# A two-layer attention kernel in one core: the engines' loop of 13 trips is written out

## The reference

```
# layer 0
h = group_norm(x, 32 groups) * gn_w + gn_b
q, k, v = split(qkv_w @ h + qkv_b)          # 128 channels each
a = softmax(q^T k / sqrt(128))              # 1024 x 1024 for each image
x = x + proj_w @ (v a^T) + proj_b
# layer 1
q, k, v = Wq @ x + bq, Wk @ x + bk, Wv @ x + bv   # q, k: 16 channels, v: 128
out = gamma * (v softmax(q^T k)^T) + x
```

## Time and profile before

| | |
|---|---|
| time, median of 3 runs | 1760.5 us (1756.99 to 1760.75) |
| time of the profiled execution | 1758.94 us |
| its span, first to last instruction | 1757.2 us |
| mean granted TensorE clock | 0.964 of full |
| PE busy | 1565.0 us (89%) |
| DVE busy | 1345.7 us (77%) |
| POOL busy | 1252.4 us (71%) |
| ACT busy | 1218.9 us (69%) |

### The profile page before, as it was taken

How to read it: one execution, slowest core, us unless ns; L and a number is a source line. 1 busy time by engine, 2 the same in 40 slices (tenths; PEclk the granted TensorE clock), 3 DMA queues, 4 the chain that set the end, 5 groups by cost and what they waited for, 6 DMA issues and landing times.

```text
span 1757.2 us, 47297 instructions
## 1 busy us (share of the span) xinstructions
PE 1565.0 (89%) x16777; PEld 1170.5 (67%) x16777; DVE 1345.7 (77%) x2547; ACT 1218.9 (69%) x1697; POOL 1252.4 (71%) x1039
## 2 busy tenths in 40 slices
PE   4889999898989989898998989989899898999965
PEld 2567777676767767676766767767676676776654
DVE  2578888787878878788787878878788787888853
ACT  2477777676767767677676767767677676777753
POOL 6997778677777878677676767868678676777600
PEclk9999999999999999999999999999999999999986
DMA  2699999999998999999899999999999999999964
GB/s 56 121 176 192 191 195 190 166 197 171 190 194 163 191 178 194 165 195 190 153 201 164 191 186 166 192 165 199 160 192 189 161 194 165 191 182 189 182 119 90
DMA packets 1081092, 305.20 MB, mean 174 GB/s; under 512 B 1067952, under 2 KB 1068624, under 8 KB 1080912
## 3 DMA queue, kind: packets, MB, share of 16 engines
q1 hardware_dynamic: 1079760, 302.41, 95.6%
q10 hardware_dynamic: 1152, 0.00, 0.0%
HBM read 17.13 MB, written 16.78 MB: 19 GB/s over the span
## 4 chain that ended last, share of the span: by engine, by line
PE 47%; ACT 22%; issue 14%; DVE 13%; POOL 2%; DVEq 1%; DMA 0%; ACTq 0%; SPq 0%; POOLq 0%
DVE nmax L499 9%; PE mixed L704 8%; PE mixed L706 7%; PE mixed L705 7%; ACT prob L404 7%; ACT scores L409 7%; PE scores L665 4%; PE scores L690 4%; PE bank_w L772 3%; PE bank_t L725 3%; PE scores L667 3%; PE scores L666 3%; ACT k_odd L438 2%; ACT v_head L456 2%; PE bank_w L762 2%
## 5 line engine op out<-in xcount | busy, mean ns | idle before, releaser
L704 PE MATMUL mixed<-v_head,pt 128*128 128x129 f16 x4096 | 746.1, 227 | 66.5 <-issue 63.8
L705 PE MATMUL mixed<-v_tail,pt 128*128 128x128 f16 x4096 | 745.1, 223 | 0.0
L706 PE MATMUL mixed<-v_head,pt 128*128 128x129 f16 x4096 | 745.1, 224 | 0.0
L499 DVE TENSOR_REDUCE nmax<-scores 128x1 f32<-128x1024 f32 x512 | 603.0, 1217 | 68.1 <-PE scores L690 46.9
L312 POOL TENSOR_TENSOR rows<-prob,rows 128x1024 f16<-128x1024 f32 x256 | 545.1, 2129 | 21.3
L409 ACT ACTIVATE scores<-scores,nmax 128x1024 f32<-128x1024 f32 x256 | 278.6, 1088 | 330.4 <-DVE nmax L499 330.4
L307 POOL TENSOR_SCALAR rows<-prob 128x1024 f16<-128x1024 f32 x256 | 267.9, 1046 | 310.7 <-ACT prob L404 308.9
L704 PEld LDWEIGHTS mixed<-v_head,pt 128*128 128x128 f16 x4096 | 408.5, 100 | 72.2 <-issue 67.7
L513 DVE SCALAR_TENSOR_TENSOR rows<-scores,rows 128x1024 f16<-128x1024 f32 x256 | 313.6, 1225 | 149.6 <-ACT rows L416 149.6
L705 PEld LDWEIGHTS mixed<-v_tail,pt 128*128 128x128 f16 x4096 | 415.5, 101 | 2.6 <-issue 0.3
L706 PEld LDWEIGHTS mixed<-v_head,pt 128*128 128x128 f16 x4096 | 407.1, 99 | 0.0
(11 more groups left out here) (93 smaller groups left out, 1927.2 us busy)
## 6 DMA issues: line engine op xcount, KB each, us to landing
x_raw<-in_x_dram SPq DMA_DIRECT2D x32, 512.0 KB, 4.9
out_dram<-y SPq DMA_DIRECT2D x64, 256.0 KB, 2.7
pt<-rows SPq DMA_TRANSPOSE x512, 4.6
w_qkv<-in_L_conv_qkv_w_dram SPq DMA_DIRECT2D x3, 64.0 KB, 3.8
w_proj<-in_L_conv_proj_w_dram SPq DMA_DIRECT2D x1, 64.0 KB, 3.7
w_v<-in_L_conv_Wv_dram SPq DMA_DIRECT2D x1, 64.0 KB, 3.6
b_qk<-in_L_conv_bk_dram SPq DMA_DIRECT2D x4, 0.1 KB, 2.4
b_qk<-in_L_conv_bq_dram SPq DMA_DIRECT2D x2, 0.1 KB, 3.1
```

What stands on the lines that cost most here:

```text
L499: nc.vector.reduce_max(nmax[layer][:, t:t + 1], scores[layer][:, :], AX.X, negate=True).then_inc(maxed[layer], 1)
L704: mm(mixed[l][:, 0:C + 1], head, vh[:, im.p, m, 0:C + 1], start=(m == 0), stop=False)
L705: mm(mixed[l][:, 0:C], head, vt[:, im.p, m, :], start=False, stop=False)
L706: done = mm(mixed[l][:, 0:C + 1], tail, vh[:, im.p, m, 0:C + 1], start=False, stop=(m == TILES - 1))
```

## The change

The loop on the engines goes away. `every_iteration` now writes all iterations from -1 to 34 out, so that each engine's program holds all of them; image numbers are constants everywhere. The order of the instructions on each engine and all waits stay as they are in the source. SP, POOL, ACT, DVE and PE all call the new form.

```diff
-LOOP = (2, 15)
...
-def every_iteration(engine, body):
-    for it in range(FIRST_IT + 1, 2 * LOOP[0]):
-        body(whole(it))
-    with engine.Fori(LOOP[0], LOOP[1]) as pair:
-        body(Image(pair, 0))
-        body(Image(pair, 1))
-    for it in range(2 * LOOP[1], LAST_IT + 1):
+def every_iteration(body):
+    for it in range(FIRST_IT + 1, LAST_IT + 1):
         body(whole(it))
...
-            every_iteration(pe, body)
+            every_iteration(body)
```

More of the change, by code:

```diff
@@ L271, in _ @@
                 sp.dma_start(b1_qk[r:r + CQK, :], col(src)).then_inc(setup_loaded, 16)
-            every_iteration(sp, body)
+            every_iteration(body)
             for h in range(2):
@@ L393, in _ @@
             body(whole(FIRST_IT))
-            every_iteration(pool, body)
+            every_iteration(body)
         @block.scalar
@@ L492, in _ @@
             act.wait_ge(consts_made, 10)
-            every_iteration(act, body)
+            every_iteration(body)
         @block.vector
@@ L657, in _ @@
             setup()
-            every_iteration(dve, body)
+            every_iteration(body)
         @block.tensor
```

## The result

The kernel with everything written out takes 1682.16 us in the median of four runs (1680.64 to 1683.96), against 1760.62 us before, the median of four runs too. The ratio is 0.9556, with a 95% interval of 0.9535 to 0.9577. The forecast was 1684, from 1675 to 1698.

What follows compares the result with a forecast made beforehand. PE, with 89% busy the leading engine, was held up by 12 taken jumps of its loop; 26 x 49.45 = 1285.7 for 1361.1, 75.4 us less, gave 1683.5 for the profiled execution and 1684 as forecast, range 1675 to 1698.

Steps and rivals of the forecast that it cites:

- A taken jump on PE costs 6.6 us: At PE's loop branch, line 84: each taken jump costs 6.6 us, clock included, 79.3 us for 12.
- the place is innocent: End of every second iteration on PE: the taken branch costs, not the place; the fall-through there idles only 0.28 us.
- The step of the sum: PE's 12 jumps go: 12 x 6.6 = 79.3 us come off the path that sets the end.
- The split of the 6.6 us: Each PE jump: about 5.6 us idle, the rest of the 6.6 from the slow restart.
- the slow restart: PE after each stop: granted clock at 0.50 for about 4 us, adding something over 1 us to each jump.
- Written-out iterations take 49.45 and not 49.30: Former loop's 26 iterations: 0.15 us slower each, 3.9 us in all, seemingly from line 672's separate wait before layer 0's scores.
- More fetches for the other four cost nothing: ACT, DVE, POOL, SP: up to 72 more q14 packets, hidden; rival: mild 1691 to 1705, full 2015, most of slower's 0.05.
- The DMA queue: Rival: DMA becomes the limit, mild 1689 to 1710, full near 1759; shares 0.11 for mild losses, 0.03 for no change.
- The clock: Rival: PE's full clock not granted so long without pauses, near 1696; shares 0.11 with mild queue and fetch losses.
- the estimate from the 108 ns: Rule against the forecast: 12 compare-and-branches at about 0.108 us, 1.3 us for the whole change; rejected for PE's trace.
- The median: Whole kernel: profiled execution 1683.5 us, median 1.6 above it at 1685, set at 1684.

Runs made afterwards that it cites:

- e1: Only PE written out, SP, POOL, ACT and DVE keep their loops, against the kernel before: 1681.11 us, ratio 0.9551.
- e3: All five engines loop over a body of four iterations with six trips, five jumps on PE instead of 12: 1712.81 us, ratio 0.9727 to the kernel before.
- e5: Everything written out, plus 12 two-trip loops of one semaphore increment on PE where the jumps were: 1685.66 us, ratio 0.9576 to the kernel before.
- e2: Only PE keeps its loop, the other four engines are written out, against the kernel before: 1750.38 us, ratio 0.9951.
- e6: The kernel before, with its loop, without the matmuls of `attend` on `v_tail`, so PE's body has 1727 instructions: 1727.58 us.
- e9: Everything written out, then four-trip loops of semaphore increments, 100 to 1100 on PE and 100 to 700 on ACT; branch durations were read, no total time given.
- e7: Everything written out, without the matmuls of `attend` on `v_tail`: 1668.12 us.
- e4: The changed kernel with PE's wait for `exped` ahead of those for `x1_done` and `y_done` in some steps: 1678.30 us, ratio 0.9532 to the kernel before.
- e11: The changed kernel with PE's `exped` wait moved ahead, measured again beside the changed kernel on one chip: 1676.68 us, ratio 0.9528 to the kernel before.
- e12: Only PE written out, with its `exped` wait moved ahead, the other four engines loop: 1678.22 us, ratio 0.9529 to the kernel before.

## Why the prediction was right

**A taken jump on PE costs 6.6 us, and the place is innocent: right, shown.** PE alone gives the gain (e1), five jumps cost about in proportion (e3: 1712.8 - 1682.2 = 30.7 us more than the changed kernel; with 24 x 0.15 = 3.6 us that its looped iterations save, 34.3 for five, 6.9 each by the medians, 7.6 each in its trace), and branches to code at hand take 0.23 us at most (e5). The step of the sum was 79.3 us for 12. So 6.6 us is the mean of this kernel's 12 jumps and no fixed price: in its own trace they cost 4.9 to 7.5 us. The forecast took that mean from the very jumps that were to go, and it needed no more.

**Its parts.** The stop is a fetch: bodies too large to stay at hand are brought anew, and packets arrive within it (e2, e6, e9). The split of the 6.6 us, 5.6 for the stop and "the rest" for the slow restart, was mis-sized, which the total hides. PE's busy time fell by 25.2 us, 2.1 for each jump, where I had said 1 to 2. The 8 us behind the restart at the first, second and sixth jump of the kernel before, in the windows view (columns as in the earlier trace rows), show it directly:

```profile
313.15:321.15 8.00, 7.99 (x66) 6.72 (x67) 1.27 (x3) 1.21 (x3) 5.41 (x5) 0.68 1.15 183
417.96:425.96 8.00, 7.99 (x86) 6.73 (x87) 2.41 (x4) 2.02 (x4) 6.04 (x5) 0.83 1.03 178
836.32:844.32 8.00, 7.99 (x74) 6.73 (x75) 1.71 (x4) 1.32 (x4) 4.08 (x4) 0.74 1.03 183
```

At a mean granted clock of 0.68, 8 busy us are short of 0.32 x 8 = 2.6 us of work; at 0.83 it is 1.4, at 0.74 it is 2.1. The first two jumps isolate the clock: their stops are alike (4.3 and 4.4 us), and the iterations behind them take 55.40 and 54.37 us (the first is in the earlier trace rows). Of the 1.2 us between the two losses of work, 1.0 shows in the time.

The idle time before the first load is 5.55 us in the mean of the 12 and the work lost at half clock 2.0; together 7.5, of which 6.6 show. The other 0.9 us seems to be taken up by PE's own ordinary waits. An iteration without a jump has 2.1 us in which PE is not busy (47.22 busy of 49.30), and in the one behind the first jump the scores' weight loads waited for the exponential for 1.6 us, where it was 2.6 in the one before. For each of the 12 jumps, and for those of e2 and e3, the trace gives the same sum, idle time plus lost work (half of the time at the lower level) less 0.9 to 1.0 us; e3's 7.6 us are 5.8 and 2.7 less 0.9.

In e6 PE has 7.8 us of such waits (40.98 busy of 48.80). Its loop costs 59.5 us, to which 26 x 0.17 = 4.4 come for e7's slower written-out iterations (48.96 us against 48.79): in all 63.9, 5.3 for each jump. Its trace has 5.25 us of idle time and 1.8 of lost work for each, so 1.8 us is taken up there. So the slow restart costs about 2 us of work after each stop, and how much of that and of the stop reaches the time is a matter of PE's slack.

**Written-out iterations take 49.45 and not 49.30: right, and its cause shown.** 1285.64 us for 26, with 1285.7 in the sum. The cause, a wait met last that sits one instruction ahead of the weights load, was called "seems"; e4 and e11 moved that wait and got iterations of 49.30 us, which is 31 x 0.14 = 4.3 us by their number; the medians fell by 3.9 and 6.3. This is the one part of the change that works against it.

**More fetches for the other four cost nothing: right but for one stop.** q14 went to 70 packets, where I had said 91 or fewer; q8 to 135 (137). The price is not quite nothing. In the changed kernel one iteration takes 49.72, and ACT's timeline has a stop that the iteration before has not:

```profile
1199.41 1.09 ACT L403 ACTIVATE scores<-scores,nmax 128x1024 f32<-128x1024 f32 x1 [1.50 <-DVE nmax L493]
1200.87 1.02 ACT L410 ACTIVATE rows<-scores 128x1024 f16<-128x1024 f32 x1 [0.37 <-ACT scores L403]
```

```profile
1149.97 1.09 ACT L403 ACTIVATE scores<-scores,nmax 128x1024 f32<-128x1024 f32 x1 [1.50 <-DVE nmax L493]
1151.15 1.02 ACT L410 ACTIVATE rows<-scores 128x1024 f16<-128x1024 f32 x1
```

Line 410 follows line 403 by 1.46 us in place of 1.18. This 0.28 us came, in this same iteration, in every kernel here in which all engines are written out, and in neither of the two in which PE alone is and ACT keeps its loop (e1, e12). It is what a fixed boundary in ACT's code would do; that it is one was not tested.

**The rivals.** The DMA queue did not become the limit: at a share of 1.09 it kept 49.45 for 26 iterations, and `attend` waited no more than before. The clock was granted for 1286 us on end. And the estimate from the 108 ns that the Trainium skill ("Advanced Engine Details and Errata", Control Flow Timing) gives for a compare-and-branch, 1.3 us in all, was off by the factor 60 for these jumps; the branches of ACT (45 ns) and near jumps on PE (0.21 to 0.23 us) lie within a factor of 2.4 of it. What tells the two kinds apart in these runs is how many instructions lie between the branch and its target (e5, e9 against e6 and the kernel before).

**The median.** I set 1684 and it is 1682.2, within the scatter of the runs that I had named. The profiled execution took 1683.15, with 1683.5 in the sum.

## What to carry to other kernels

Look in a trace for idle time whose releaser is "issue" and that comes once in a loop's trip; the compare-and-branch of that engine, or the gap right behind it (ACT in e9), then says whether the jump waits for code. Write out the loop on the engine that has the long body and leave it on the others: here PE's 12 jumps were worth 79 us, and those of four other engines nothing. Where constants take the place of registers, see which wait ends up on the instruction itself: the one that is met last should stand first in the source here, so that no wait instruction runs behind it (e11, 1676.7 us, is the fastest kernel here that leaves nothing of the computation out).

## What the runs showed of the hardware that was not expected

The price of a taken jump has steps. It was 0.21 us on PE for bodies of 100 to 1100 instructions and 4.2 us or more for 1727 and 2239; the edge between was not tried, nor whether increments and matmuls differ. The loop of e6 fetched more packets than the same iterations written out (112 against 85). It may be that code beyond the branch is fetched too and takes room from the body; that was not tested. On ACT it was 0.2 us up to 300 and some 2.4 us from 500 on, with DMA engines otherwise idle, and this stop is in no branch record: it stands before the next one. On PE it is in the branch's own duration, and in the kernel before it had two sizes, near 4.3 us with one 16 KB packet on its way and near 5.9 with two (e3's stop of 6.1 us had one).

The Trainium skill ("Runtime: NRT & Kernel Launch", Instruction fetch mechanics) gives 512 instructions for most engines and 2048 for PE as what fits. The first is only roughly borne out, as ACT's body of 500 increments did not stay and its edge lies between 300 and 500; the second does not agree with PE's body of 1727, which was fetched anew on each trip.

After a stop of PE its granted clock is at 0.50, the 1.2 GHz level, and this took 1.4 to 2.6 us of work from the 8 us behind the stops shown above, for stops of like length too.

And the compiler's joining of waits is visible in time: when the wait instruction (two waits in one, 51 ns) runs after the last event and not before it, the scores start 0.06 us later (0.63 against 0.57 in the earlier trace rows), and an iteration, with two such places, takes 0.14 us more.
